# Attention outputs written by feature and not normalised, divided later in the dense stages; 4+3 PSUM banks for maxima and scores

## The chip, the cores and the metric

The kernel runs on one core of a Trainium2 chip. The metric is the device time of one execution in microseconds; the profiled execution is one such execution, and the trace quoted below is its trace. Engines: PE is TensorE, PEld its weight loads, DVE is VectorE, ACT is ScalarE, POOL is GpSimd, SP is SyncE, which issues every DMA of this kernel.

## The reference

The input x is (2, 2048, 256) in float32. There are 16 heads of 16 features.

```python
x = x + attn_a(layernorm(x))   # qkv = x @ W_attn; causal softmax; att * decay; y @ W_proj
x = x + ffn(layernorm(x))      # weights replaced by mean|w| * sign(w), exact gelu, 256 -> 1024 -> 256
x = x + attn_b(layernorm(x))   # biased q, k, v; causal softmax; o @ Wo + bo; layernorm * gamma + beta
x = x + ffn(layernorm(x))
```

In both attentions a query's output is a sum over keys of weight times value, divided by the sum of the weights. In the first the numerator's weights are multiplied by a table that falls with the distance and is 0 from 512 on, while the denominator sums all keys.

## The kernel before, in words

Six stages run one after the other, with a barrier between them: `setup` (signs of the FFN weights), `projections` (q, k, v of attention A), `attention` "att_a" (decayed), `dense` "mid" (A's output projection, FFN, q, k, v of attention B), `attention` "att_b", and `dense` "end" (B's output projection, its layernorm, FFN). They pass data through DRAM.

**attention** (L544 to L923) works on 8 groups (2 sequences by 4 groups of 4 heads), on 4 chunks of 512 queries each. Two passes are interleaved by a written-out order, `attention_plan` (L456): for group g it runs scores and outputs, and beside them the maxima of the rest of g and of the first part of g+1. All engines walk the same list of items, each taking what is its own:
- "M": scores of 128 queries by up to 512 keys (PE, L860) into one of `MBANKS` banks of PSUM, and their row maximum (DVE, L782, L786). In att_a the keys that the decay leaves out also get "FX" (ACT, L749): exponentials summed into `fsum`, later corrected and added up into `ftotal` (L806, L809).
- "MC": the maxima are turned by DVE (L815) and written into the operand `qop` by DMA (L672), so that the scores come out shifted.
- "S": scores by key block (PE, L882) into one of `EBANKS` banks, exponentials (ACT, L742), in att_a the decay (POOL, L704).
- "PO" and "PV": sums of weights and weighted values, four heads in four strips of 32 partitions of the one bank `po` (L900, L907, L917). A strip holds 16 features and then rows with the sum of weights.
- "O": ACT copies `po` to `y` (L762). "YT": PE turns `y` by four transposes into the bank `px` (L869). "YN": DVE adds `ftotal` where there are far keys (L823), takes the reciprocal of a 128x16 tile (L825, L827), scales 128x256 values (L831), and SP stores them (L677), one DMA a chunk.

PSUM has 8 banks: 4+2 for maxima and scores in att_a, 3+3 in att_b, and one each for `po` and `px`.

**dense** (L1005 to L1434) works on 8 chunks of 512 rows, in the order of `dense_plan` (L934), which all engines walk. Its items: "Y" loads y (L1074), turns it by 8 transposes (PE, L1214) and copies it to `yt` (ACT, L1304); "P" projects (PE, L1232; DVE adds the residual, L1386, or the bias, L1380); "S", "N" and "T" are moments on DVE (L1348 on) with the normalising on POOL (L1143, L1151); "A" is a residual sum (DVE, L1395); "X" and "Z" are transposes; "H" is one of 8 blocks of the FFN's first matrix (PE, L1250; ACT's gelu, L1316; DVE splits it in two, L1409, L1411); "O" is its part of the second matrix (PE, L1261), which needs DVE's L1411; "B" and "R" turn back and add (L1269, L1419); "Q" and "V" are the next q, k, v. In mid, Y of chunk G+2 stands in the list after the third O of chunk G; in end, Y of chunk G+3 stands after the last O of chunk G and after "N". The list of either opens with a prologue:

```python
    plan = [("Y", 0), ("P", 0), ("S", 0), ("Y", 1)]
    if not qkv:
        plan += [("A", 0), ("N", 0)]
    plan += [("P", 1), ("S", 1), ("X", 0)]
    if not qkv:
        plan += [("A", 1), ("N", 1), ("Y", 2)]
    plan += [("H", 0, h) for h in range(EARLY)]
```

SP loads the first two chunks of y and x, the weights, and in mid last `wqkv`, `bqk` and `bv` (L1093 to L1097). In mid, DVE waits for these (`qkv_in`, L1366) before its first item.

## Time and profile before

| | us |
|---|---|
| median of 3 runs | 2737.45 (2736.65 to 2740.8) |
| profiled execution, its own time | 2736.11 |
| its span, first to last instruction | 2734.4 |
| PE busy | 2454.8 (90%) |
| DVE busy | 1958.3 (72%) |
| ACT busy | 1515.6 (55%) |
| POOL busy | 1052.5 (38%) |
| mean granted TensorE clock | 0.959 of full |

A busy time is the time in which an instruction of the engine is under way; PE's counts pipelined matmuls with modelled ends, so it is not work at its peak. A wait names the instruction that released it. Between two stages all engines stop.

### The profile page before, as it was taken

To read this page: it belongs to the slowest core of one execution; us is meant where nothing else is said; L and a number is where in the kernel's file an instruction comes from. 1 tells how busy PE (TensorE), PEld (TensorE's weight loads), DVE (VectorE), ACT (ScalarE), POOL (GpSimd) and SP (SyncE) were. 2 spreads that over 40 slices of the span, in tenths; PEclk is the share of its full clock that TensorE was granted. 3 is DMA by queue.
4 is the path that set the end of the run, shared out by engine and by line. 5 is a ranking of instruction groups with operands and counts; after the bars stand their busy time and mean duration, and the time that the engine had idled before them with its cause. 6 is when DMAs were issued, how large, how long until landed. Compare 5 with 4: busy or idle time off the path is not lost. (4 is left out here: it accounts for less than half of the span.)

```text
span 2734.4 us, 44488 instructions
## 1 busy us (share of the span) xinstructions
PE 2454.8 (90%) x13984; PEld 1404.0 (51%) x13984; DVE 1958.3 (72%) x4863; ACT 1515.6 (55%) x3309; POOL 1052.5 (38%) x1274
## 2 busy tenths in 40 slices
PE   4959999999999999969997599999999999997788
PEld 2535545454544545437774355555555555553676
DVE  5667787777787777716663588888888888870786
ACT  1218576776767685734332056666666666664333
POOL 0037777777777777751221301000101001011653
PEclk8969999999999999989998589999999999998999
DMA  4994142332505050033544751423505234102110
GB/s 134 252 144 63 24 56 36 44 51 32 70 11 75 13 69 6 5 114 77 125 96 98 111 75 16 64 38 44 70 15 72 32 51 62 18 7 99 47 54 31
DMA packets 181847, 171.03 MB, mean 63 GB/s; under 512 B 90352, under 2 KB 131056, under 8 KB 180848
## 3 DMA queue, kind: packets, MB, share of 16 engines
q1 hardware_dynamic: 181616, 168.18, 35.0%
q8 instruction: 116, 1.90, 0.3%
q14 instruction: 115, 0.94, 0.2%
HBM read 105.98 MB, written 61.08 MB: 61 GB/s over the span
## 5 line engine op out<-in xcount | busy, mean ns | idle before, releaser
L704 POOL TENSOR_TENSOR att_a_wd<-att_a_wt,decay 128x256 f32<-128x256 f32 (+3 forms) x896 | 754.6, 873 | 259.8 <-PE att_a_po L907 122.7
L742 ACT ACTIVATE att_b_wt<-att_b_ps 128x512 f32<-128x512 f32 (+3 forms) x1280 | 589.4, 539 | 354.6 <-PE att_b_ps L882 352.6
L782 DVE TENSOR_REDUCE att_a_mpart<-att_a_pm 128x1 f32<-128x512 f32 x768 | 513.5, 687 | 132.2 <-PE att_a_pm L860 129.0
L782 DVE TENSOR_REDUCE att_b_mpart<-att_b_pm 128x1 f32<-128x512 f32 x768 | 503.7, 686 | 109.7 <-PE att_b_pm L860 107.7
L860 PE MATMUL att_a_pm<-att_a_kop,att_a_qop 128*128 128x512 f32 (+3 forms) x1280 | 522.6, 426 | 55.6 <-DMA att_a_qop<-att_a_qop 28.2
L742 ACT ACTIVATE att_a_wt<-att_a_ps 128x512 f32<-128x512 f32 (+3 forms) x896 | 430.8, 506 | 218.1 <-PE att_a_ps L885 131.6
L860 PE MATMUL att_b_pm<-att_b_kop,att_b_qop 128*128 128x512 f32 (+3 forms) x1280 | 503.0, 408 | 36.6 <-DMA att_b_qop<-att_b_qop 29.9
L882 PE MATMUL att_b_ps<-att_b_qop,att_b_kop 128*128 128x512 f32 (+3 forms) x1280 | 453.2, 383 | 6.6 <-ACT att_b_wt L742 3.4
L722 POOL TENSOR_SCALAR_AFFINE_SELECT att_b_wt<-att_b_wt 128x512 f32<-128x512 f32 x128 | 81.6, 637 | 867.1 <-ACT att_b_wt L742 867.1
L860 PEld LDWEIGHTS att_a_pm<-att_a_kop,att_a_qop 128*128 128x128 f32 x1280 | 240.6, 193 | 324.6 <-DVE att_a_mpart L782 130.2
L860 PEld LDWEIGHTS att_b_pm<-att_b_kop,att_b_qop 128*128 128x128 f32 x1280 | 246.3, 194 | 277.1 <-DVE att_b_mpart L782 112.0
L882 PE MATMUL att_a_ps<-att_a_qop,att_a_kop 128*128 128x512 f32 (+3 forms) x896 | 324.2, 370 | 6.2 <-ACT att_a_wt L742 6.1
L749 ACT ACTIVATE att_a_pm<-att_a_pm,att_a_mpart 128x512 f32<-128x512 f32 x384 | 255.2, 665 | 95.5 <-DVE att_a_mpart L782 92.7
L917 PE MATMUL att_b_po<-att_b_wt,att_b_va 128*17 128x512 f32 (+3 forms) x2560 | 296.6, 535 | 11.0 <-ACT att_b_y L762 7.8
L786 DVE CUSTOM_DVE_ANT_0 att_a_pm<-att_a_pm,late 128x384 f32<-128x384 f32 (+3 forms) x512 | 248.3, 498 | 69.2 <-PE att_a_pm L860 69.1
L882 PEld LDWEIGHTS att_b_ps<-att_b_qop,att_b_kop 128*128 128x128 f32 x1280 | 234.2, 189 | 118.8 <-ACT att_b_wt L742 84.2
L786 DVE CUSTOM_DVE_ANT_0 att_b_pm<-att_b_pm,late 128x384 f32<-128x384 f32 (+3 forms) x512 | 248.5, 498 | 50.4 <-PE att_b_pm L860 49.2
L900 PE MATMUL att_a_po<-att_a_wt,ones_strip 128*32 128x512 f32 (+3 forms) x1792 | 198.6, 515 | 18.9 <-ACT att_a_y L762 18.9
L882 PEld LDWEIGHTS att_a_ps<-att_a_qop,att_a_kop 128*128 128x128 f32 x896 | 169.9, 190 | 75.3 <-ACT att_a_wt L742 63.4
L907 PE MATMUL att_a_po<-att_a_wd,att_a_va 128*16 128x256 f32 (+3 forms) x1792 | 164.1, 438 | 3.3 <-POOL att_a_wd L704 3.3
L885 PE MATMUL att_a_ps<-mask_k,identr 128*128 128x128 f32 x512 | 118.7, 236 | 0.0
L1143 POOL TENSOR_TENSOR mid_rs<-mid_var,mid_power 128x4 f32<-128x4 f32 x16 | 17.6, 1098 | 234.5 <-DVE mid_var L209 234.5
(174 smaller groups left out, 2622.6 us busy)
## 6 DMA issues: line engine op xcount, KB each, us to landing
att_a_kop<-qk SPq DMA_DIRECT2D x128, 128.0 KB, 7.7
att_a_qop<-qk SPq DMA_DIRECT2D x128, 128.0 KB, 8.0
att_b_kop<-qk SPq DMA_DIRECT2D x128, 128.0 KB, 6.2
att_b_qop<-qk SPq DMA_DIRECT2D x128, 128.0 KB, 6.8
qk<-qkv_a_qk_hi SPq DMA_DIRECT2D x32, 256.0 KB, 4.7
qk<-qkv_a_qk_lo SPq DMA_DIRECT2D x32, 256.0 KB, 4.5
qk<-mid_qk_hi SPq DMA_DIRECT2D x32, 256.0 KB, 4.0
qk<-mid_qk_lo SPq DMA_DIRECT2D x32, 256.0 KB, 4.5
```

Of the source, the lines that this page charges most:

```text
L704: pool.tensor_tensor(wd[:, kq % 2, j, a:z], wt[:, kq % buffers, j, a:z], keep["decay"][:, u:u + z - a], ALU.mult).then_inc(w_decayed, 1)
L722: pool.affine_select(out=block, in_=block, compare_op=ALU.is_ge, fill=0.0, base=0, pattern=[[0, GH], [1, P]], channel_multiplier=-1).then_ ...
L742: act.activation(wt[:, kq % buffers, j, a:CH], pe_[:, seen % EBANKS, 0:CH - a], ACT.Exp)\
L749: act.activation(pm[:, n % MBANKS, :], pm[:, n % MBANKS, :], ACT.Exp, bias=mpart[:, c, piece, u:u + 1], accum_out=fsum[:, c, piece, u:u + ...
L782: dve.tensor_reduce(mpart[:, c, piece, u:u + 1], pm[:, n % MBANKS, 0:w], AX.X, ALU.max, negate=True).then_inc(m_reduced, 1)
L786: dve.tensor_tensor_reduce(out=pm[:, n % MBANKS, 0:w], in0=pm[:, n % MBANKS, 0:w], in1=keep["late"][:, CH - w:CH], scale=-1.0, scalar=-2 * ...
L860: mm = pe.matmul(pm[:, bank, 0:w], qop[:, mpar, c, j, qb * P:(qb + 1) * P], kop[:, mpar, j, piece * CH:piece * CH + w], start=True, stop=True)
L882: mm = pe.matmul(pe_[:, bank, 0:CH - a], kop[:, par, j, kb * P:(kb + 1) * P], qop[:, par, c, j, a:CH], start=True, stop=not diagonal)
L885: mm = pe.matmul(pe_[:, bank, 0:P], keep["identr"][:, :], keep["mask_k"][:, :], start=False, stop=True)
L900: mm = pe.matmul(po[STRIP * j:STRIP * (j + 1), a:CH], keep["ones_strip"][:, :], wt[:, ones % buffers, j, a:CH], start=first, stop=False)
L907: mm = pe.matmul(po[STRIP * j:STRIP * j + VW, a:z], va[:, par, kb, j, :], wd[:, kq % 2, j, a:z], start=False, stop=last)
L917: mm = pe.matmul(po[STRIP * j:STRIP * j + VW, a:CH], va[:, par, kb, j, :], wt[:, kq % buffers, j, a:CH], start=first, stop=last)
```

## The change

Both attentions no longer transpose or divide their output. "YT" and "YN" are gone from the plan. At "O" ACT copies `po` into one of two buffers `y`, and SP stores it as it lies, 8 DMAs a chunk (for each head 16 feature rows, and one row of sums). In att_a the far sums are turned by DVE, 16 at a time ("FT"), and stored by 4 DMAs to a tensor of their own. The bank `px` goes to the others: 4+3 in both attentions. In the dense stages y comes by feature, so PE's transposes and ACT's copy of "Y" are gone. Instead SP loads each head's sums spread over 16 partitions (16 DMAs a chunk, 16 more where there are far sums, that is in mid for chunks 2, 3, 6 and 7, which POOL adds), and DVE takes the reciprocal of 128x1024 values and multiplies.

```diff
 def attention_plan(...):
-            follow(number + 3, GH - 1, ("YT", c))
...
-    return [x for item in plan for x in ((item, ("YN", *item[1:])) if item[0] == "YT" else (item,))]
+    return [item for _, _, _, item in sorted(timed)]
 def spaced(m, decayed):
-                follow((8, 0.0, ("FE", c)), (11, 0.0, ("FM", c)))
+                follow((8, 0.0, ("FE", c)), (11, 0.0, ("FM", c)), (14, 0.0, ("FT", c)))
 def attention(...):
-        MBANKS, EBANKS = (4, 2) if decayed else (3, 3)
+        MBANKS, EBANKS = 4, 3
...
+        y = sb("y", [P, 2, CH], F32)
+        pm, pe_, po = ps("pm", [P, MBANKS, CH]), ps("ps", [P, EBANKS, CH]), ps("po", [P, CH])
...
         SP:
+                    if item[0] == "FT":
+                        sp.wait_ge(f_turned, len(FARS) * (g + d) + n + 1)
+                        for k in range(P // SQUARE):
+                            sp.dma_start(to[:, k, :], frow[SQUARE * k:SQUARE * k + UNITS, n, :]).then_inc(f_out[n], 16)
-                    if item[0] == "YN":
+                    if item[0] == "O":
+                        sp.wait_ge(o_kept, done(g, c) + 1)
+                        for j in range(GH):
+                            sp.dma_start(dram["y"][g // NG, h, :, cols], y[STRIP * j:STRIP * j + HD, c % 2, :])\
+                              .then_inc(y_out[c % 2], 16)
+                            sp.dma_start(dram["sums"][g // NG, h:h + 1, cols],
+                                         y[STRIP * j + HD:STRIP * j + HD + 1, c % 2, :]).then_inc(y_out[c % 2], 16)
...
         ACT, item "O":
+                        act.wait_ge(y_out[c % 2], Y_DMAS * (2 * g + c // 2 + 1))
+                        act.activation(y[:, c % 2, :], po[:, :], ACT.Copy).then_inc(o_kept, 1)
...
         DVE:
+                    if item[0] == "FT":
+                        dve.transpose(frow[:, n, :], ftotal[:, n, :]).then_inc(f_turned, 1)
-                    if item[0] == "YN":  (L816 to L832)
         PE:
-                    if item[0] == "YT":  (L863 to L870)
 def dense(...):
             def load_y(G):
                 if G >= 2:
-                    sp.wait_ge(y_turned, G - 1)
+                    sp.wait_ge(yt_ready, G - 1)
+                sp.dma_start(y[:, G % 2, :, :], dram["y"][b].rearrange("(k h) d t -> (h d) k t", k=KT)[:, :, cols])\
+                  .then_inc(y_in[G % 2], 16)
+                for h in range(H):
+                    sp.dma_start(sums[part, G % 2, h // (H // KT), :],
+                                 dram["sums"][b, h:h + 1, cols].to_broadcast([HD, CH])).then_inc(y_in[G % 2], 16)
+                if G in FAR_CHUNKS:
+                    if n:
+                        sp.wait_ge(sums_ready, n)
+                    for h in range(H):
+                        sp.dma_start(far_sums[part, h // (H // KT), :], row_of(row).to_broadcast([HD, CH]))\
+                          .then_inc(far_in, 16)
...
         POOL:
+                if item[0] == "Y" and G in FAR_CHUNKS:
+                    pool.tensor_tensor(sums[:, G % 2, :, :], sums[:, G % 2, :, :], far_sums[:, :, :], ALU.add)\
+                        .then_inc(sums_ready, 1)
         PE:
-                if item[0] == "Y":  (transposes, L1221 to L1224)
         ACT:
-                if item[0] == "Y":  (copy, L1300 to L1304)
         DVE:
+                if item[0] == "Y":
+                    dve.wait_ge(y_in[par], Y_LOADS * (G // 2 + 1))
+                    if G in FAR_CHUNKS:
+                        dve.wait_ge(sums_ready, FAR_CHUNKS.index(G) + 1)
+                    if G:
+                        dve.wait_ge(projected, G)
+                    dve.reciprocal(sums[:, par, :, :], sums[:, par, :, :]).then_inc(inverted, 1)
+                    dve.wait_ge(inverted, G + 1)
+                    dve.tensor_tensor(yt[:, :, :], y[:, par, :, :], sums[:, par, :, :], ALU.mult).then_inc(yt_ready, 1)
```

## Rows read from the trace of the kernel before

**Rows 1.** Windows by stage: us, busy time and instructions of PE, PEld, DVE, ACT, POOL, clock, DMA

```profile
168.00:1188.00 1020.00, 961.19 (x6360) 505.64 (x6360) 780.20 (x1989) 696.61 (x1709) 760.19 (x896) 0.98 0.31 41
1520.00:2498.00 978.00, 928.08 (x5224) 487.66 (x5224) 758.24 (x1924) 602.71 (x1308) 101.31 (x138) 0.96 0.33 46
```

**Rows 2.** Windows of one steady chunk of mid and one of end, columns as in Rows 1

```profile
1269.70:1303.60 33.90, 32.73 (x146) 24.03 (x145) 21.33 (x49) 13.22 (x17) 8.17 (x13) 1.00 0.58 121
2603.30:2627.50 24.20, 21.77 (x106) 17.15 (x104) 19.87 (x43) 9.42 (x12) 13.76 (x15) 1.00 0.20 66
```

**Rows 3.** Timeline, end, a steady chunk: start us, us, engine, line, instruction, [idle before <-releaser]

```profile
2625.43 0.42 DVE L1409 CAST end_g_hi<-end_g 128x512 fp32r<-128x512 f32 x1
2626.64 0.73 PE L1261 MATMUL end_po<-end_g_hi,end_w_signs 128*128 128x512 f32 x2 [0.28 <-DVE end_g_lo L1411]
```

**Rows 4.** Groups by line: the output transposes of the attentions, busy, mean ns, idle before

```profile
L869 PE MATMUL att_b_px<-ident,att_b_y 128*128 128x128 f32 x128 | 20.0, 279 | 3.1 <-ACT att_b_y L762 3.1
L869 PE MATMUL att_a_px<-ident,att_a_y 128*128 128x128 f32 x128 | 19.6, 275 | 2.7 <-ACT att_a_y L762 2.7
```

**Rows 5.** Timeline of PE in a steady stretch of att_b

```profile
2005.60 0.62 PE L869 MATMUL att_b_px<-ident,att_b_y 128*128 128x128 f32 x4
2005.97 0.47 PE L860 MATMUL att_b_pm<-att_b_kop,att_b_qop 128*128 128x512 f32 x1
```

**Rows 6.** Waits: who waited for whom, total us, times, longest us

```profile
PEld att_b_pm L860 <- DVE att_b_mpart L782: 112.0, 241, 0.9
PEld att_a_ps L882 <- ACT att_a_wt L742: 63.4, 121, 2.4
```

**Rows 7.** Timeline, issues of SP: a load of 16 partitions, the spread load of bv

```profile
158.39 0.43 SPq L646 DMA_DIRECT2D att_a_kop<-qk  x1
1209.09 0.71 SPq L1097 DMA_DIRECT2D mid_bv<-in_L_attn_b_bv  x1
```

**Rows 8.** Groups by line: reciprocals and whole-chunk elementwise work on VectorE

```profile
L323 DVE RECIPROCAL qkv_a_rs<-qkv_a_sd 128x4 f32<-128x4 f32 x8 | 1.4, 178 | 2.3 <-ACT qkv_a_sd L377 2.3
L825 DVE RECIPROCAL att_a_inverse<-att_a_sums 128x16 f32<-128x16 f32 x16 | 4.0, 253 | 0.6
L1395 DVE TENSOR_TENSOR end_x<-end_zg,end_xb 128x1024 f32<-128x1024 f32 x8 | 9.7, 1215 | 10.6 <-POOL end_zg L1171 10.6
L771 DVE MEMSET att_a_mneg<- 128x64 f32 x1 | 0.1, 112 | 0.1
L1163 POOL TENSOR_TENSOR end_xb<-end_x,end_beta 128x1024 f32<-128x1024 f32 x8 | 19.3, 2409 | 9.5 <-DMA end_beta<-in_L_attn_b_beta 9.5
```

**Rows 9.** Timeline, opening of mid

```profile
1197.57 0.36 SPq L1074 DMA_DIRECT2D mid_y<-y  x1
1204.72 5.53 PE L1232 MATMUL mid_pp<-mid_wp,mid_yt 128*128 128x256 f32 x16 [1.21 <-ACT mid_yt L1304]
1214.88 0.17 DVE L1367 TENSOR_SCALAR mid_bqk<-mid_bqk 128x2 f32<-128x2 f32 x1 [20.36 <-DMA mid_bv<-in_L_attn_b_bv]
1227.98 0.47 PE L1250 MATMUL mid_ph<-mid_xt_hi,mid_w_signs 128*128 128x512 f32 x1 [4.00 <-DVE mid_xt_lo L1401]
```

**Rows 10.** Timeline, a steady chunk of mid

```profile
1294.78 0.69 DVE L1411 TENSOR_TENSOR mid_g_lo<-mid_g,mid_g_hi 128x512 fp32r<-128x512 f32 x1
1300.02 3.62 PE L1232 MATMUL mid_pp<-mid_wp,mid_yt 128*128 128x256 f32 x16
1301.19 1.40 DVE L1348 BATCH_NORM_STATS2 mid_stats<-mid_x 128x6 f32<-128x256 f32 x4
1303.32 0.16 DVE L209 SCALAR_TENSOR_TENSOR mid_var<-mid_half 128x4 f32<-128x4 f32 x1
1307.84 1.09 PE L1214 MATMUL mid_pt<-ident,mid_xn 128*128 128x128 f32 x8 [0.53 <-POOL mid_xn L1151]
```

**Rows 11.** Timeline, opening of end: the first load, and the first product with W2

```profile
2506.47 0.36 SPq L1074 DMA_DIRECT2D end_y<-y  x1
2551.68 0.74 PE L1261 MATMUL end_po<-end_g_hi,end_w_signs 128*128 128x512 f32 x2 [2.62 <-DVE end_g_lo L1411]
```

More of the change, by code:

```diff
@@ L862, in step @@
                         mm.then_inc(m_scores, 1)
-                    if item[0] == "YT":
-                        c = item[1]
-                        pe.wait_ge(o_kept, done(g, c) + 1)
-                        if done(g, c) > 1:
-                            pe.wait_ge(y_ready, done(g, c) - 1)
-                        for t in range(TB):
-                            mm = pe.transpose(px[:, t * P:(t + 1) * P], y[:, t * P:(t + 1) * P], keep["ident"][:, :])
-                        mm.then_inc(y_turned, 1)
                     if item[0] == "S":
@@ L1066, in dense @@
         N_W = 16 * (1 + 3 * bool(norm))
+        Y_LOADS, F_LOADS = 16 * (1 + H), 16 * H
+        FAR_CHUNKS = [G for G in range(CHUNKS) if decayed and far(G % NC, decayed)]
         N_QKV = 16 * (len(weights) + 3) if qkv else 0
@@ L1197, in wait_turned @@
                     what, G = BEFORE[item]
-                    if what == "Y":
-                        pe.wait_ge(yt_ready, G + 1)
-                    elif what == "X":
+                    if what == "X":
                         pe.wait_ge(hi_ready, G + 1)
@@ L1459, in build @@
             "v": dram("v", (B, NG, NC, P, TB * GH * (HD + 1)), F32),
-            "y": chunks(dram("y", (B, T, D), F32)),
+            "y": dram("y", (B, H, HD, T), F32),
+            "sums": dram("sums", (B, H, T), F32),
+            "far": dram("far", (B, NG, NC, UNITS, P), F32),
             "w1s": dram("w1s", (P, KT, FF), F32), "w2s": dram("w2s", (P, HT, D), F32),
@@ L1480, in build @@
         attention(nc, "att_b", False, keep, scratch)
-        dense(nc, "end", x[1], x[2], t["L0_attn_b_Wo"], [t[f"L0_attn_b_{n}"] for n in ("bo", "gamma", "beta")],
+        dense(nc, "end", x[1], x[2], t["L0_attn_b_Wo"], False, [t[f"L0_attn_b_{n}"] for n in ("bo", "gamma", "beta")],
               None, None, keep, scratch)
```

88 lines of the change are left out of this document (39 added, 49 removed).

## The prediction

> **What bounds the kernel now.** I read the windows by stage first, since an average over stages hides what each part of the change meets. The two attentions hold 1998 of 2734 us. In both PE has something under way for 94% and 95% of the time, DVE for 76% and 78% [rows 1]: PE sets the pace, so work taken off PE counts, and work taken off DVE counts only through what PE waits for. Next came the windows of one chunk of each dense stage. In mid PE is busy 32.7 of 33.9 us, DVE 21.3. In end PE is busy 21.8 and DVE 19.9 of 24.2 us [rows 2], and the timeline says that DVE is the one behind: PE stands waiting for L1411, the split of a gelu block, right after DVE has come out of its moments [rows 3]. So end is paced by DVE and PE in turns, and anything that holds DVE at that place holds PE.
>
> The change thus takes work from PE in the stages that PE bounds, and puts work on DVE in the stages where DVE is near the bound or in the way. Sums are made against the profiled execution, 2736.1 us; the median of the runs is 1.3 us above it. About 0.2% (5.5 us) is what a measurement of this kernel can tell from no change.
>
> **Attentions: transposes and division.** There are 64 chunks (8 groups by 4 chunks, twice), each with 4 transposes. From the first of them to the next instruction of PE is 0.37 us [rows 5], so 64 x 0.37 = 24 us, plus PE's idle time before them, 3.1 + 2.7 us [rows 4]: **-30**. Their busy time, 20.0 and 19.6 us, overlaps the neighbours and would be the upper price (-45). DVE's adds, reciprocals and scalings go too, some 0.8 us a chunk; PE is the bound, so they are costed at nothing beyond the waits of the next part. DVE's 16 transposes of the far sums come in their place, about 0.2 us each by the transpose of the maxima, hidden in the same way.
>
> **Attentions: banks.** att_a gets a third scores bank, att_b a fourth maxima bank. The waits that they bear on are PE's weight loads for ACT's exponentials (63.4 us in att_a) and for DVE's maxima (112.0 us in att_b) [rows 6]. A weight load may be early, so most of such a wait lies beside the matmul before it. Bounds: 0 (PE had other work), and all the time in which PE has nothing under way, 59 + 50 us [rows 1], less the 6 already counted, so -103. I take a third: **-36**, nearer the lower end, as the waits are 0.5 us on average and PE is over 94% busy.
>
> **Attentions: stores.** SP issues 8 DMAs a chunk for one, 0.43 us each by the nearest row, a DMA of 16 partitions [rows 7]. That is 3.4 us of SP in some 30 us, plus 4 small ones for each of the 16 far chunks. Behind them on SP stand the writes of the maxima into qop (L672) and the next group's loads; SP is mostly waiting there, so they cost nothing, and if that cover is gone PE's first score of a chunk waits for L672. At the end of a stage there is no cover: 7 more issues are 3.0 us, less about 1.5 for the transposes and division that stood there. Twice: **+3**.
>
> **What Y costs on DVE.** This decides the case. Reciprocals of 4 elements a partition take 178 ns and of 16 take 253 [rows 8]: 75 ns for 12 elements, 6.25 ns each, over a fixed 153. For 1024 elements that is 153 + 1024 x 6.25 = 6550 ns. An addition of the same size takes 1.22 us for all of it [rows 8], so a reciprocal pays about five times as much per element. With the multiplication, 1.22, and a gap, Y is **7.85 us** of DVE, 16 times. Bounds: 2.5 us, if a long reciprocal ran as an addition; and 10.3, if the fixed part were only the 112 ns of the shortest memset [rows 8], since (253 - 112) / 16 = 8.8 ns, 9.1 us for 1024. I take 7.85, because it alone fits both sizes of this very operation.
>
> The Trainium skill's page "VectorE: DVE Perf Modes" (First, the fixed hardware budget) says that the reciprocal is an iterated division with a repeat count of 8. Eight cycles at the 0.96 GHz of that page would be an estimate of 8.3 ns an element, where the rows give 6.25; what that would make of the time is a rival below.
>
> **Opening of mid.** SP issues everything in order. Y of chunks 0 and 1 becomes 17 DMAs each, so 32 more stand ahead of `bv`, the last thing that DVE waits for. Before, the first load went out at 1197.6, `bv` at 1209.1, and DVE started at 1214.9 [rows 7, 9]. Now there are about 45 issues, at 0.43 to 0.46 us some 21 us and 1 us for the slower ones, so `bv` goes out near 1220 and DVE starts near 1225: +10 (bounds +3, if the issues before were waiting for data, as 8.7 us for the last seven suggest, to +20 at the 0.71 of `bv` [rows 7]). Then DVE's Y stands in line. Before, the projection of chunk 0 was long done when DVE began, and the first FFN block ran 13.1 us later [rows 9]. Now Y(0) comes first, then the projection, 5.53 us [rows 9], then Y(1): 7.85 + 5.53 + 7.85 = 21. Together **+31**.
>
> **Steady mid.** Y(G+2) follows a split that ended at 1295.5 [rows 10], so it ends at 1303.3. PE goes on meanwhile with blocks whose splits are done, and loses its own Y transposes; then it stands before P(G+2), which began at 1300.0. That is 3.3 late. DVE then has two splits, R and the moments T to do; T ran from 1301.2 to 1303.5 [rows 10] and would now end near 1309.0 (1303.3 + 1.1 + 1.2 + 1.1 + 2.3). POOL normalises from T, and PE's Z, at 1307.84, waited for it already by 0.5 us [rows 10]. So Z and all after it slip by **5.5** a chunk, six times (chunks 2 to 7): **+33**. What is late next is POOL's chain from T to Z. DVE had 12.6 us of slack a chunk [rows 2], which is why not all 7.85 shows. POOL's addition of the far sums, 2.4 us [rows 8], four times, lies where POOL waits anyway; if DVE's two-input work collides with it, it costs up to 2 us each.
>
> **Opening of end.** The first load goes out at 2506.5 [rows 11]; 17 issues (7.5) and a landing (2 to 3) bring the data by 2516.5. I replay the list with 5.5 for a projection, 3.6 for an addition and its moments (1.2 + 2.3), and about 6 for POOL's chain (1.0 + 0.2 + 2.2 for normalising, 2.4 for gamma). Y(0) to 2524, P(0) to 2530, S(0) to 2533, Y(1) to 2541 with POOL's chain beside it, A(0) and N(0) to 2545 with P(1) beside, S(1) to 2550, X(0) to 2553, A(1) and N(1) to 2560 after POOL's second chain, Y(2) to 2567.5, the split to 2568.6. Then PE's first product with W2 starts; before it was at 2551.7 [rows 11]: **+17** (10 to 22).
>
> **Steady end.** Y(G+3) stands between the moments N and the split that PE is waiting for [rows 3]. Nothing of it is hidden: PE's next product waits all of it, then R, then P, which needs R's banks. The chain after it is the same as before, shifted. The floor is DVE's own work, 19.9 + 7.85 against 24.2, so +3.5; the ceiling is 7.85. I take 7.7, five times (chunks 3 to 7): **+38**. After such a wait PE's clock is low: the projection took 5.53 us after a wait and 3.62 in full swing [rows 9, 10]. It follows close on the stall and lies on the path: 1.5 us five times, **+8** (0 to 10).
>
> **Sum.** -30 - 36 + 3 = -63 for the attentions; 31 + 33 = +64 for mid, 17 + 38 + 8 = +63 for end. Together +64: 2736.1 + 64 = 2800.
>
> **Rivals.**
> (a) *The long reciprocal is cheap* (Y is 2.5 us). Then mid's opening costs 10 + 2.5 + 5.5 + 2.5 = 20.5, its six chunks gain 1.4 each (the transposes and the wait before them), end pays 3 + 5 x 2.5 = 15.5: +27 in all, against -63: 2700. For it: every other DVE operation here pays about 1.2 ns an element. Against: two sizes of the same operation [rows 8]. Between 2700 and 2800 the sum crosses zero where Y is about 4.4 us. Chance 0.08.
> (b) *The banks free PE fully*: -103 instead of -36 gives 2733, just faster or the same. For it: DVE and ACT have 20% and more to spare in both attentions. Against: every step there goes in fixed order, and no wait of PE is long. Chance 0.08, half of it faster.
> (c) *A long reciprocal costs more an element than the short ones*: Y at the upper bound's 8.8 ns is 10.3 us, 2.4 more, and all 16 lie on the path: 2800 + 39 = 2839. Against: the slope of 6.25 between two sizes [rows 8]. Chance 0.12. (By the page's eight cycles, in the Trainium skill's "VectorE: DVE Perf Modes", the estimate would be 2.1 more for each, 2834.)
> (d) *SP becomes the bound in mid*. A far chunk has 33 loads, 12 stores and 2 more; at 0.43 this is 20 us of 39, at 0.71 33 us, and the loads wait in order behind `yt_ready`. If spread loads issue slower still, DVE waits for y: another 20 to 35 us, 2825. Against: SP's unhindered issues are all near 0.43. Chance 0.12.
> (e) *The banks bring nothing*: 2836. Chance 0.06.
>
> **How the numbers follow.** The forecast has 0.54; the rivals 0.08, 0.08, 0.12, 0.12, 0.06. Its own range, from the bounds of the two openings, of the banks and of the end chunks, is 2765 to 2830. The range 2744 to 2845 leaves out (a), (b) and the top of the slower cases. Faster: (a) and half of (b), 0.12 less what is left of them within 0.2%: 0.11. Same: 0.03. Slower: 0.86.
>
> **What would show it.** Right: a reciprocal of 128x1024 near 6.5 us, 16 of them; PE waiting in end for L1411 by 7 us right after; mid's DVE starting near 1225 less what att_a gained; mid some 64 us longer, end some 63; each attention some 30 shorter, with no L869, and PE's waits for L782 and for L742 smaller. Wrong: a reciprocal near 1.2 us (a); attentions shorter by over 50 each (b); SP issuing without a pause through mid while DVE waits for a DMA of sums (d).

## The result, and the profile after

The changed kernel takes **2834.7 us** (median of 4 runs, 2831.0 to 2837.7) where the kernel before takes 2738.0 (2736.7 to 2740.8): a ratio of 1.0351, with a 95% interval of 1.0333 to 1.0369. That is 97 us slower. The forecast was 64 us slower, 2800 us, and its range of 2744 to 2845 holds the result. The profiled execution took 2837.7 us, with a span of 2836.0 and a mean granted clock of 0.929.

I cut the span into stages at the first load that each stage issues. The stage starts of the changed kernel, from SP's queue in the timeline (start us, us, engine, line, instruction):

```profile
155.83 0.33 SPq L648 DMA_DIRECT2D att_a_kop<-qk  x1
1174.19 0.38 SPq L1077 DMA_DIRECT2D mid_y<-y  x1
1584.10 0.34 SPq L648 DMA_DIRECT2D att_b_kop<-qk  x1
2536.56 0.38 SPq L1077 DMA_DIRECT2D end_y<-y  x1
```

The same cuts in the kernel before lie at 156.6, 1197.6, 1531.2 and 2506.5. So each stage took, in us:

| stage | before | after | difference | forecast |
|---|---|---|---|---|
| first attention | 1041.0 | 1018.4 | -22.6 | -31 |
| mid | 333.7 | 409.9 | +76.3 | +64 |
| second attention | 975.3 | 952.5 | -22.8 | -31 |
| end | 227.9 | 299.4 | +71.5 | +63 |

A stage that an edit doesn't touch varies between executions by about 1 to 3 us (the second attention by 7), so differences of a few us in one stage say little.

Windows of the changed kernel, columns as in [rows 1]: the attentions, then one steady chunk of mid and one of end, which answer to [rows 2].

```profile
168.00:1165.00 997.00, 947.75 (x6238) 492.64 (x6239) 763.65 (x1928) 691.85 (x1709) 758.71 (x895) 0.98 0.33 43
1596.00:2529.00 933.00, 906.28 (x5103) 482.70 (x5103) 730.58 (x1856) 600.99 (x1308) 89.31 (x132) 0.97 0.34 46
1319.90:1360.60 40.70, 33.63 (x138) 24.72 (x137) 28.54 (x53) 12.33 (x17) 7.46 (x12) 0.92 0.56 129
2663.20:2697.20 34.00, 23.97 (x97) 18.24 (x96) 27.21 (x45) 8.49 (x11) 12.32 (x14) 0.85 0.22 62
```

PE is busy for 95.1% of the first attention's window, where it was 94.2%. The second attention needs care: its window before, in [rows 1], opens at 1520, while the stage's first load goes out at 1531.2 and its first matmul starts at 1543.05:

```profile
1543.05 7.20 PE L860 MATMUL att_b_pm<-att_b_kop,att_b_qop 128*128 128x128 f32 x16 [28.52 <-DMA att_b_qop<-att_b_qop]
```

So 23 of the 50 us without PE work that [rows 1] shows there are the stage's opening. From 1543.2 to 2498 PE was busy for 97.2%, and it is 97.1% now: that attention is shorter because PE has less under way, not because it idles less. In the dense stages PE waits more than before. A chunk of mid went from 33.9 to 40.7 us with PE busy for 33.6 us where it was 32.7, and DVE is busy for 28.5 us of it, 7.2 more than before. A chunk of end went from 24.2 to 34.0, with 7.3 us more of DVE and a granted clock of 0.85 where it was 1.00.

**What Y costs.** The groups by line (busy us, mean ns of one | idle before), which answer to the estimate from [rows 8]:

```profile
L1393 DVE RECIPROCAL mid_sums<-mid_sums 128x1024 f32<-128x1024 f32 x8 | 52.4, 6547 | 0.0
L1393 DVE RECIPROCAL end_sums<-end_sums 128x1024 f32<-128x1024 f32 x8 | 52.4, 6551 | 61.4 <-DMA end_sums<-sums 61.4
L1395 DVE TENSOR_TENSOR mid_yt<-mid_y,mid_sums 128x1024 f32<-128x1024 f32 x8 | 9.8, 1225 | 0.3
L1180 POOL TENSOR_TENSOR mid_sums<-mid_sums,mid_far_sums 128x1024 f32<-128x1024 f32 x4 | 9.6, 2402 | 0.0
```

The reciprocal is 6.55 us, as forecast, and the multiplication 1.22.

**Opening of mid**, timeline, to be held against [rows 9]:

```profile
1202.15 6.55 DVE L1393 RECIPROCAL mid_sums<-mid_sums 128x1024 f32<-128x1024 f32 x1
1210.11 5.80 PE L1249 MATMUL mid_pp<-mid_wp,mid_yt 128*128 128x256 f32 x16 [41.31 <-DVE mid_yt L1395]
1227.29 5.76 PE L1249 MATMUL mid_pp<-mid_wp,mid_yt 128*128 128x256 f32 x16 [11.38 <-DVE mid_yt L1395]
1237.92 0.47 PE L1267 MATMUL mid_ph<-mid_xt_hi,mid_w_signs 128*128 128x512 f32 x1 [4.00 <-DVE mid_xt_lo L1422]
```

DVE's first Y, Y(0), starts 28 us after the stage's first load, P(0) comes after it, then Y(1), then P(1). The first FFN block comes 63.7 us after the first load; before it came after 30.4.

**A steady chunk of mid**, to be held against [rows 10]:

```profile
1319.88 6.55 DVE L1393 RECIPROCAL mid_sums<-mid_sums 128x1024 f32<-128x1024 f32 x1
1322.35 0.61 PE L1278 MATMUL mid_po<-mid_g_lo,mid_w_signs 128*128 128x512 f32 x2
1326.46 1.23 DVE L1395 TENSOR_TENSOR mid_yt<-mid_y,mid_sums 128x1024 f32<-128x1024 f32 x1
1328.66 1.22 DVE L1440 TENSOR_TENSOR mid_x<-mid_pp,mid_x 128x1024 f32<-128x1024 f32 x1
1330.03 5.58 PE L1249 MATMUL mid_pp<-mid_wp,mid_yt 128*128 128x256 f32 x16 [7.07 <-DVE mid_x L1440]
```

PE ends its last product with W2 at 1322.96 and then stands for 7.07 us. What it needs is R (L1440), which empties the banks of `pp` and stands behind Y and one split on DVE. Then the projection P takes 5.58 us, at a granted clock of 0.66 in the window 1330.0 to 1335.6; before it took 3.62, at 1.00 [rows 10]. PE's waits of 0.5 us before, for POOL's normalised x at Z, and of 0.6 us for DVE are gone.

**A steady chunk of end**, to be held against [rows 3]:

```profile
2663.16 6.55 DVE L1393 RECIPROCAL end_sums<-end_sums 128x1024 f32<-128x1024 f32 x1
2672.09 1.22 PE L1278 MATMUL end_po<-end_g_hi,end_w_signs 128*128 128x512 f32 x2 [8.00 <-DVE end_g_lo L1432]
2673.11 1.05 PE L1278 MATMUL end_po<-end_g_lo,end_w_signs 128*128 128x512 f32 x2
2674.38 5.83 PE L1249 MATMUL end_pp<-end_wp,end_yt 128*128 128x256 f32 x16 [0.22 <-DVE end_x L1440]
```

Here PE's product with W2 waits 8.00 us for the split behind Y. The products after the stall take 1.22 and 1.05 us where such a pair of matmuls takes 0.62 to 0.73 in the steady chunks before the change, and the projection 5.83 where those chunks had 3.69. The granted clock is 0.50 from 2672.0 to 2674.4, 0.62 from 2674.4 to 2680.0 and 1.00 in the 4 us behind; "the low clock" below means the level of 0.50, for the whole of a stretch or for a part of it. The slow products cost nothing here: from the start of the first to the start of the projection it is 2.29 us now and was 2.29 us before (2626.64 to 2628.93), as the projection waits for R on DVE in both. So a chunk's 9.85 us more are 7.7 of stall (8.00 for 0.28 us) and 2.1 of the projection.

### The profile page after: what moved, and what is told of

The parts are those of the page before. It is cut to its first block and busy times, and to the rows that moved or that the text cites. A ratio compares the mean times of both kernels' runs of the same rounds, so it can differ in the third digit from the quotient of the medians.

```text
span 2836.0 us, 44312 instructions
## 1 busy us (share of the span) xinstructions
PE 2430.7 (86%) x13600; PEld 1390.1 (49%) x13600; DVE 2038.0 (72%) x4768; ACT 1495.0 (53%) x3293; POOL 1047.8 (37%) x1278
## 5 line engine op out<-in xcount | busy, mean ns | idle before, releaser
L866 PE MATMUL att_a_pm<-att_a_kop,att_a_qop 128*128 128x512 f32 (+3 forms) x1280 | 511.2, 425 | 59.9 <-DMA att_a_qop<-att_a_qop 28.6
L866 PE MATMUL att_b_pm<-att_b_kop,att_b_qop 128*128 128x512 f32 (+3 forms) x1280 | 486.6, 401 | 36.8 <-DMA att_b_qop<-att_b_qop 30.8
L880 PE MATMUL att_b_ps<-att_b_qop,att_b_kop 128*128 128x512 f32 (+3 forms) x1280 | 460.7, 386 | 12.2 <-DMA att_b_qop<-att_b_mrow 7.1
L866 PEld LDWEIGHTS att_a_pm<-att_a_kop,att_a_qop 128*128 128x128 f32 x1280 | 239.1, 194 | 309.3 <-DVE att_a_mpart L799 131.7
L866 PEld LDWEIGHTS att_b_pm<-att_b_kop,att_b_qop 128*128 128x128 f32 x1280 | 246.2, 195 | 252.5 <-DVE att_b_mpart L799 108.6
L880 PEld LDWEIGHTS att_b_ps<-att_b_qop,att_b_kop 128*128 128x128 f32 x1280 | 238.4, 189 | 129.5 <-ACT att_b_wt L757 77.8
L880 PEld LDWEIGHTS att_a_ps<-att_a_qop,att_a_kop 128*128 128x128 f32 x896 | 170.5, 191 | 84.5 <-ACT att_a_wt L757 71.1
L1328 ACT ACTIVATE end_g<-end_ph,b,alpha 128x512 f32<-128x512 f32 x64 | 49.9, 779 | 168.8 <-PE end_ph L1267 164.1
L1328 ACT ACTIVATE mid_g<-mid_ph,b,alpha 128x512 f32<-128x512 f32 x64 | 49.9, 779 | 155.2 <-PE mid_ph L1267 155.2
```

Of the source, the lines that this page charges most:

```text
L866: mm = pe.matmul(pm[:, bank, 0:w], qop[:, mpar, c, j, qb * P:(qb + 1) * P], kop[:, mpar, j, piece * CH:piece * CH + w], start=True, stop=True)
L880: mm = pe.matmul(pe_[:, bank, 0:CH - a], kop[:, par, j, kb * P:(kb + 1) * P], qop[:, par, c, j, a:CH], start=True, stop=not diagonal)
L1328: act.activation(g[:, h % GB, :], ph[:, BANK[item], :], ACT.Gelu, bias=keep["b1"][:, h:h + 1], scale=keep["alpha1"][:, h:h + 1]).then_inc( ...
```

## The experiments

All are edits of the changed kernel, but for the control. The table gives the median of all runs, the ratio to the kernel before (to runs of it made beside each kernel, with medians of 2738.0 to 2738.9) with its interval, and the stages of the profiled execution, cut as above (us).

| kernel | median | ratio | att_a | mid | att_b | end |
|---|---|---|---|---|---|---|
| before | 2738.0 | 1 | 1041.0 | 333.7 | 975.3 | 227.9 |
| changed | 2834.7 | 1.0351 [1.0333, 1.0369] | 1018.4 | 409.9 | 952.5 | 299.4 |
| no reciprocal | 2725.9 | 0.9954 [0.9935, 0.9974] | 1018.5 | 349.1 | 946.6 | 254.5 |
| banks of before | 2856.7 | 1.0424 [1.0407, 1.0441] | 1026.8 | 410.8 | 963.7 | 298.4 |
| other banks | 3012.9 | 1.0991 [1.0973, 1.1010] | 1090.9 | 411.5 | 1052.5 | 299.0 |
| four pieces | 2811.5 | 1.0277 [1.0246, 1.0308] | 1018.5 | 397.2 | 952.2 | 285.8 |
| scaling later | 2816.8 | 1.0276 [1.0259, 1.0293] | 1018.2 | 392.5 | 953.4 | 298.4 |
| Y of end after S | 2822.6 | 1.0304 [1.0286, 1.0323] | 1018.1 | 408.6 | 946.6 | 286.1 |
| Y of mid after block 6 | 2846.3 | 1.0395 [1.0380, 1.0410] | 1016.8 | 420.8 | 952.5 | 298.5 |
| compact inverse | 2734.8 | 0.9984 [0.9970, 0.9997] | 1026.2 | 343.6 | 951.8 | 252.7 |
| compact, two orders | 2716.4 | 0.9912 [0.9895, 0.9928] | 1026.3 | 332.8 | 955.1 | 244.4 |
| and two spread loads | 2707.1 | 0.9886 [0.9871, 0.9900] | 1026.7 | 327.8 | 952.2 | 240.9 |
| control: before, scaling later | 2734.2 | 0.9983 [0.9975, 0.9992] | 1042.8 | 327.1 | 974.4 | 231.2 |

### No reciprocal

```
-                    dve.reciprocal(sums[:, par, :, :], sums[:, par, :, :]).then_inc(inverted, 1)
-                    dve.wait_ge(inverted, G + 1)
```

> The changed kernel without its 16 long reciprocals: Y multiplies by the sums, so the division is left out. Theory (a reciprocal lies on the path with its whole 6.55 us, and PE's low clock behind the stall with 1.5 to 2 us): both openings shorter by 13 and 14 us, mid's steady chunk 33.5 instead of 40.7 us (six times, -43), end's steady chunk 26 instead of 34.0 us (five times, -40): about -110, 2725 us. Rival 1 (the 17 to 33 loads of a chunk through SP, or the place of Y in the order, cost by themselves): at most half of it comes back, 2780 us or more. Rival 2 (the reciprocal costs its duration and nothing more, 16 times): -95 to -105 with the projection still at 5.4 us after a wait, 2735 us.

Measured: 2725.9 us, 109 less than the changed kernel, where the 16 reciprocals last 104.8 together. The theory's 2725 holds in the sum, and rival 1 (at most half comes back) falls. The theory's parts fit less well: mid gave 60.8 us where 56 were expected and end 45.0 where 54 were, and 5.9 us come from the second attention, which the edit leaves alone. So the sum alone does not tell the theory from rival 2, by which a reciprocal costs its duration and nothing more; the stages and the projections do. The projections, on PE in the timeline, a chunk of mid and one of end:

```profile
1294.81 3.69 PE L1249 MATMUL mid_pp<-mid_wp,mid_yt 128*128 128x256 f32 x16 [0.49 <-DVE mid_x L1438]
2611.22 5.33 PE L1249 MATMUL end_pp<-end_wp,end_yt 128*128 128x256 f32 x16 [1.35 <-DVE end_x L1438]
```

In mid the stall is down from 7.07 to 0.49 us, the projection is back at 3.69 (granted clock 1.00), and a chunk takes 32.4 us (from the starts of R), 1.5 less than before the change. In end a chunk takes 27.2 us, 3.0 more than before, and the projection stays at 5.33, at a granted clock of 0.68, as rival 2 had it. Two short stalls stand ahead of it, 1.43 for a split and 1.35 for R, where the kernel before had 0.28 and 1.10 and a projection of 3.69. So one multiplication of 1.22 us at that place goes with 3.0 us more a chunk, of which 1.6 are the slow projection.

### The banks

```
-        MBANKS, EBANKS = 4, 3
+        MBANKS, EBANKS = (4, 2) if decayed else (3, 3)
```

> The changed kernel with the banks of before: 4 for maxima and 2 for scores in the first attention, 3 and 3 in the second. The rest of the change stays. The attentions got 45 us shorter together where 63 was forecast. Theory (the banks are worth only what is left after 30 for the transposes): +15 to +18, 8 in each attention, 2852 us, with PE's waits for the exponentials and the maxima nearly unchanged in number. Rival 1 (the banks are worth the 36 of the forecast, and the stores cost some 20): +36, 2871 us. Rival 2 (the banks are worth nothing, and the transposes cost 45 with their busy time): 2835 us, no change.

Measured: 2856.7, 22 us more than the changed kernel, from 8.4 in the first attention and 11.2 in the second. This is nearer the theory (2852) than either rival (2871 and 2835). What is left between this kernel and the kernel before is the removal of the transposes and of the division, with the new stores: -14.2 and -11.6, together -26, where the forecast had -30 + 3. So these two terms were right in their sum (no run takes them apart), and the banks' was not. The second attention varies by up to 7 us between kernels that are the same there, so its 11.2 and 11.6 are rough; the two medians, 2856.7 and 2834.7, confirm some 20 us for both banks. The waits of this kernel (us in total, times, longest):

```profile
PEld att_b_pm L866 <- DVE att_b_mpart L799: 130.4, 252, 0.9
PEld att_a_ps L880 <- ACT att_a_wt L757: 98.9, 193, 1.4
```

and of the changed kernel:

```profile
PEld att_b_pm L866 <- DVE att_b_mpart L799: 108.6, 161, 0.9
PEld att_a_ps L880 <- ACT att_a_wt L757: 71.1, 104, 1.2
```

The extra bank takes 21.8 us off the first wait and 27.8 off the second, and the stages got 11.2 and 8.4 shorter, a half and a third of that. Against the kernel before [rows 6], 112.0 and 63.4, the waits of the changed kernel hardly fall or even rise: without its transposes PE comes earlier to the same waits. Only these two kernels, which differ in the banks alone, show what a bank is worth. PE's time from a stage's first matmul to the stage's end, by windows of the three traces (us with an instruction under way, us without):

| kernel | first attention | second attention |
|---|---|---|
| before | 964.5, 64.8 | 930.9, 32.5 |
| banks of before | 962.1, 52.8 | 922.4, 29.3 |
| changed | 950.1, 56.2 | 907.6, 32.9 |

With the extra bank the time without an instruction does not fall, it rises by 3.4 and 3.6 us; what falls is the time under way, by 12.0 and 14.8. The weight loads' waits for a bank, 130.4 us for the maxima of the second attention alone, are longer than the 29.3 us without an instruction there, so most of them lie beside matmuls that count as under way.

Then the splits on the other side:

```
-        MBANKS, EBANKS = 4, 3
+        MBANKS, EBANKS = (3, 4) if decayed else (5, 2)
```

> The changed kernel with other splits of the seven banks: 3 for maxima and 4 for scores in the first attention, 5 and 2 in the second. Read by stage. Theory (each attention is within a few per cent of PE's own work, and 4 and 3 is near the best): both attentions longer, the first by 5 to 15 us, the second by 3 to 15: 2850 us. Rival (the waits for the maxima, the larger ones in the second attention, show that banks for maxima are what it lacks): the second attention shorter by 5 or more.

Measured: +72.5 in the first attention and +100.0 in the second. The theory expected 5 to 15 and 3 to 15 us. The direction was right, but the sizes are some 5 and 7 times the tops of these ranges. The rival (the second attention shorter by 5 or more) falls. Waits:

```profile
PEld att_b_ps L880 <- ACT att_b_wt L757: 252.5, 658, 1.0
PEld att_a_pm L866 <- DVE att_a_mpart L799: 200.1, 315, 1.5
PE att_a_pm L866 <- ACT att_a_pm L764: 46.3, 113, 1.0
```

With two banks for scores in the second attention, PE's weight loads wait 658 times for an exponential, 252.5 us where it was 77.8 (157 times). The first attention, with two banks for scores, lost only 8.4; with three for maxima it loses 72. There PE waits 200.1 us for DVE's maxima (131.7 in the changed kernel) and 46.3 us for ACT's exponentials of the far scores, which also hold these banks (8.3). So of the splits tried 4 and 3 is the best for both attentions, but two banks can be nearly enough in one stage and far too few in the other.

### The reciprocal in four pieces

The items `("I", G, k)` take a piece of 256 elements each and stand between earlier splits; the multiplication stays where Y was.

```
+                if item[0] == "I":
+                    k = item[2]
...
+                    part = sums[:, par, k // 2, k % 2 * 256:k % 2 * 256 + 256]
+                    dve.reciprocal(part, part).then_inc(inverted, 1)
```

> The changed kernel with each reciprocal cut into four of 256 elements (1.75 us each by the fixed part and slope, 7.0 in all), which stand one by one at earlier places of the order, between the splits of the FFN blocks; the multiplication stays where Y was. VectorE has the same work and 0.5 us more a chunk. Theory (in mid it is the stall of PE behind one long instruction that costs, VectorE has 12 us of slack there; in end the sum of VectorE's work is nearly the bound): mid's chunk 35 to 36 instead of 40.7 us, end's chunk 29 to 30 instead of 34.0: -50, 2785 us. Rival (the amount of VectorE's work decides, not the length of one instruction): within 10 us of the changed kernel, 2835 to 2845 us.

Measured: 2811.5, 23 less than the changed kernel and not 50. Both stages gave about 13 us. Rows of two chunks of mid and one of end, from the timeline:

```profile
1369.38 1.75 DVE L1407 RECIPROCAL mid_sums<-mid_sums 128x256 f32<-128x256 f32 x1 [2.88 <-POOL mid_sums L1188]
1339.13 5.37 PE L1309 MATMUL mid_ph<-mid_xt,mid_wqkv 128*128 128x512 f32 x8 [3.31 <-DVE mid_qk_lo L1459]
2688.58 5.33 PE L1257 MATMUL end_pp<-end_wp,end_yt 128*128 128x256 f32 x16 [3.08 <-DVE end_x L1452]
```

A piece takes 1.75 us, so the slope from 256 to 1024 elements is (6.55 - 1.75) / 768 = 6.25 ns, and the fixed part 0.15: the same line as between 4 and 16 elements. In a near chunk of mid (1320.7 to 1358.2) PE waits only 0.7 us before the projection, which is back at 3.69. But the chunk takes 37.5 us where the kernel without a reciprocal has 32.4, because the stall has moved: PE's qkv products wait 3.31 us for DVE's split of them (L1459), which stands behind two pieces, and 8 of them then take 5.37 us at a granted clock of 0.68, where the 8 before took 3.60. A far chunk takes 41, since its first piece waits 2.88 us for GpSimd's addition. In end the projection is still slow after a stall of 3.08, and a chunk takes 31.3 to 33.3 where 29 to 30 were expected. So neither the theory nor the rival (within 10 us of the changed kernel) stands alone. Cutting the instruction gives back a fifth of what the reciprocal costs (23 of 109 us); the rest goes with the amount of work, since most of DVE's idle time in mid is time in which it owes something within a few us.

### Where Y stands

In end, after the moments S:

```
                 if h == 3 and ahead:
                     plan.append(("S", G + 2))
+                if h == 3 and G + 3 < CHUNKS:
+                    plan.append(("Y", G + 3))
...
                 if h == 7 and ahead:
                     plan.append(("N", G + 2))
-                if h == 7 and G + 3 < CHUNKS:
-                    plan.append(("Y", G + 3))
```

> The changed kernel with the full Y (reciprocal and multiplication) of end after the moments S instead of after the moments N; nothing else. Theory (6.55 us of VectorE in one instruction hold PE wherever they stand between two splits, since end has no long stretch of PE without a split): end's chunk 32.5 to 34 instead of 34.05 us: -8 to 0, 2830 us. Rival (it is the place ahead of R and P that costs): end's chunk below 31 us, -15 or more, 2820 us or less.

Measured: 2822.6, with end 13.3 us shorter; a chunk takes 31.1 to 32.6. It lies between the two. A projection in the steady stretch:

```profile
2661.94 3.61 PE L1249 MATMUL end_pp<-end_wp,end_yt 128*128 128x256 f32 x16
```

It takes 3.61, at a granted clock of 1.00, where the changed kernel has 5.83, and a chunk gained 2.3 us on average. But the low clock is not gone. The same 6.55 us of DVE still hold PE, which stands idle for 8.8 us ahead of 2649.16, and what follows the stall is now a block of the FFN and its product: these eight matmuls take 3.56 us at a granted clock of 0.50, and the next eight of the same kind take 1.87 at 0.98. So the same instructions on the same data show what the low clock costs, 2.2 us for a projection and 1.7 for a block; how the 2.3 us of a chunk divide among this and the waits is open.

In mid, Y after block 6 of the chunk, where DVE was idle:

```
-                if h == 2 and ahead:
-                    plan.append(("Y", G + 2))
+                if h == 2 and G == 0:
+                    plan.append(("Y", 2))
...
+                if h == 6 and G + 3 < CHUNKS:
+                    plan.append(("Y", G + 3))
```

> The changed kernel with Y of mid moved: Y of chunk G+3 stands after block 6 of chunk G, ahead of the transposes and the qkv products, where VectorE was idle in the changed kernel, and not before R and P, behind which PE stood 7.07 us. Same work. Theory (PE's stall and the low clock behind it are the cost, the amount of VectorE's work is not, with 12 us of slack a chunk): mid's chunk 36 to 38 instead of 40.7 us, the projection at 3.7 instead of 5.6 to 5.9: -20, 2815 us. Rival (PE's qkv products wait for VectorE's splits, so the stall moves there with all its length): mid's chunk within 1.5 us of 40.7, 2830 us or more.

Measured: 2846.3, 12 us slower than the changed kernel. My theory fell, and the rival's mechanism holds. Near chunks take 40.3 and 40.6 us, as the rival has it; the two far chunks behind them take 45.1 and 44.7, more than it allowed. Rows of a far chunk:

```profile
1373.70 3.62 PE L1251 MATMUL mid_pp<-mid_wp,mid_yt 128*128 128x256 f32 x16
1388.86 6.55 DVE L1395 RECIPROCAL mid_sums<-mid_sums 128x1024 f32<-128x1024 f32 x1 [5.09 <-POOL mid_sums L1182]
1398.54 6.01 PE L1303 MATMUL mid_ph<-mid_xt,mid_wqkv 128*128 128x512 f32 x8 [10.65 <-DVE mid_qk_lo L1449]
```

The projection is at 3.62 again and no longer waits. But DVE waits 5.09 us for GpSimd's addition of the far sums before it can take the reciprocal, and PE's qkv products then stand 10.65 us for DVE's split of them (L1449) and run at a granted clock of 0.60, 6.01 us for 8 matmuls where 8 took 3.60 at 1.00 just before. In a near chunk, without the addition, they stand 5.47 us and 8 of them take 6.35 or 6.71. DVE's idle time at this place was not free: the first of those splits was due at 1386.9, when ACT had written `qk_hi`, before the reciprocal had begun.

### The opening of mid

```
-            if qkv:
-                dve.wait_ge(qkv_in, N_QKV)
...
                 if item[0] == "S":
                     dve.wait_ge(p_read, G + 1)
                     moments(z if norm else x1[:, G % 3, :, :])
+                    if qkv and G == 1:
+                        dve.wait_ge(qkv_in, N_QKV)
...
```

> The changed kernel with one wait moved: in mid VectorE waits for the qkv weights and biases and scales them after the moments of chunk 1, no longer ahead of all its work, so Y of chunk 0 can start when its 17 loads have landed. Theory (mid's opening is late by the queue of 33 loads ahead of these weights and by two serial Y): the first FFN block 46 us after mid's first load instead of 64, the rest of mid the same: -17, 2818 us. Rival (the 16 loads of the second chunk's sums are then the next wait, and Y of chunk 1 starts no earlier): -10 or less, 2825 us or more.

Measured: 2816.8 and mid 17.4 us shorter, with the first FFN block 46.4 us after the first load. So the theory holds, and the wait for these weights, behind the queue of loads, was worth 17 us to the changed kernel. The control, the same edit in the kernel before:

> A control: the kernel before, with only the scaling of mid's qkv weights moved after the moments of chunk 1. There the projection of chunk 0 ended at 1210.2 and VectorE began its addition at 1215.4, so theory: at most 5 us, with the second projection earlier by as much: -3 to -5, 2734 us. Rival (the edit is worth as much here as the 18 us in the changed kernel): -15, 2723 us, and then most of what the fastest version gains over the kernel before is not due to the change.

Measured: 2734.2, 4 us less, as the theory has it. In the profiled executions mid is 6.6 us shorter, a little more than the theory's 5, and end, which the edit leaves alone, 3.3 longer. The wait cost little there, since P(0) did not stand behind it.

### Dividing in compact form

The sums of a group's chunk are 4 x 512 numbers, which is 16 a partition. The kernel loads them back one chunk later, adds the far sums, inverts them there, and the dense stages spread the inverses.

```
+                if q >= 4:
+                    dve.wait_ge(ci_out[q % 4], 16 * (q // 4))
+                dve.reciprocal(ci[:, q % 4, :], cs[:, q % 4, :]).then_inc(c_inverted, 1)
...
-                    dve.reciprocal(sums[:, par, :, :], sums[:, par, :, :]).then_inc(inverted, 1)
-                    dve.wait_ge(inverted, G + 1)
                     dve.tensor_tensor(yt[:, :, :], y[:, par, :, :], sums[:, par, :, :], ALU.mult).then_inc(yt_ready, 1)
```

> Another way to divide: the attentions keep the stores by feature, 4+3 banks, and no transposes of the output; one chunk later the 4x512 sums of a group are loaded back as 128x16, the far sums are added to them there, VectorE takes a reciprocal of 128x16 (0.25 us), and the inverses are stored; the dense stages spread the inverses over partitions instead of the sums and only multiply (1.22 us). No far loads or additions on GpSimd in mid. Theory: the dense stages run as without the reciprocal, and the attentions keep their gain less 5 us at the end of each for the last round trip: about 2730 us. Rival (SP's three more transfers a chunk and VectorE's waits for them hold PE in the attentions): 2760 us or more.

Measured: 2734.8 against a theory of 2730; the rival (2760 or more) falls. The end of the first attention:

```profile
1174.76 0.34 SPq L661 DMA_DIRECT2D inverse<-att_a_ci  x1
1177.04 2.15 SPq L661 DMA_DIRECT2D inverse<-att_a_ci  x3
1177.72 0.25 DVE L884 RECIPROCAL att_a_ci<-att_a_cs 128x16 f32<-128x16 f32 x1
```

32 reciprocals of 0.25 us an attention take the place of 8 of 6.55. The last one has no cover: from the start of PE's last matmuls to the first load of mid it is 10.9 us, where the changed kernel has 5.8. That is 5.1 of the 7.8 us by which the first attention is longer than in the changed kernel. The second attention shows none of it beyond its variation.

Then the two orders of above in this kernel (scaling later in mid, and Y of end, now one multiplication, after S):

> The kernel with the inverses taken from 128x16 in the attentions, and two orders changed: VectorE scales the qkv weights in mid after the moments of chunk 1, and Y of end (now one multiplication) stands after the moments S instead of after the moments N, where PE waits for the split behind it. Theory: mid's opening shorter by 10 to 15; end's steady chunk back from 27.2 to 24.5 us, and the projection there at 3.7 instead of 5.3 us, since PE's stalls are short again (five times, -13): 2708 us, faster than before by 1.1%. Rival (end is held by VectorE's own work and its collisions with GpSimd, not by the place of Y): end's chunk stays at 26.5 or more, 2720 us.

Measured: 2716.4, where 2708 was expected. Mid gave 10.8 us. End gave 8.3 and not 13: a chunk takes 25.3 us, with the projection back at a granted clock of 1.00:

```profile
2581.66 3.69 PE L1298 MATMUL end_pp<-end_wp,end_yt 128*128 128x256 f32 x16
```

And the 16 spread loads of a chunk as two, with the inverses laid out by head:

```
-                for h in range(H):
...
+                for k in range(KT):
+                    rows = dram["inverse"][b, c, H // KT * k:H // KT * (k + 1), :]
+                    sp.dma_start(sums[:, G % 2, k, :],
+                                 rows.unsqueeze(1).to_broadcast([H // KT, HD, CH])).then_inc(y_in[G % 2], 16)
```

> The fastest version so far (inverses from 128x16, scaling later, Y of end after S) with one edit: the 16 spread loads of a chunk, one a head, become 2, each of 8 heads by 16 partitions by 512. Theory (SP's queue of 17 issues ahead of everything else sets both openings): first projection 5 to 6 us earlier in mid and in end, steady chunks unchanged: -11, 2705 us. Rival (a transfer of 128 rows of 2 KB from 8 rows of DRAM lands later than 8 small ones, by the bytes and not by the issues): no gain, 2716 us.

Measured: 2707.1, 9 us less. The opening of mid:

```profile
1182.53 1.37 SPq L1131 DMA_DIRECT2D mid_sums<-inverse  x2
1189.75 1.23 DVE L1436 TENSOR_TENSOR mid_yt<-mid_y,mid_sums 128x1024 f32<-128x1024 f32 x1 [10.72 <-DMA mid_sums<-inverse]
1191.12 5.99 PE L1299 MATMUL mid_pp<-mid_wp,mid_yt 128*128 128x256 f32 x16 [19.65 <-DVE mid_yt L1436]
```

Two issues take 1.37 us where 16 took 7.4, but the data are there only at 1189.75, 5.9 us after the second issue; the small ones of the kernel without this edit landed in 2.3 to 3.1 (medians of end and mid). So the first projection came 2 us earlier in mid and 4 in end, not 5 to 6, and the rival took a part of the gain there. That the total of 9 is still near the 11 of the theory has a part that it did not name: mid's second projection came 3.5 us earlier, and mid as a whole is 5.0 us shorter.

This version is 1.1% faster than the kernel before (0.9886, 0.9871 to 0.9900). Of its 31 us, 4 would come without the change, by the control. Whether the other order, Y of end after S, would gain anything in the kernel before was not tested.

## Why the prediction was right

The sign and the range held, and so did the mechanism in its main part: a reciprocal of 6.55 us on DVE holds PE, and costs the dense stages more than the attentions gain. The size was off by a third. All its misses go the same way, so that nothing cancelled. Step by step, in the stages of the two profiled executions (101.6 us between the spans, 64 forecast):

- **Transposes and division out of the attentions, stores in: -30 + 3.** Right as a sum: -26, by the kernel with the banks of before.
- **Banks: -36.** This term was mis-sized: -20. I took a third of PE's whole idle time, 59 + 50 us. That bound was read wrong: 23 of the 50 are the opening of the second attention, before its first matmul at 1543.05, and without them and the 6 already counted it is 80, a third of which is 27. (A third of the 103 that I had written is 34, not 36.) And the quantity was the wrong one: with the extra banks PE's time without an instruction rose by 3.4 and 3.6 us, and its time under way fell. What an extra bank takes off is 22 to 28 us of waits a stage, and a third to a half of it reaches the stage's end. The sign that I had named, smaller waits for L782 and L742, mostly failed: from 112.0 to 108.6 and from 63.4 to 71.1 against [rows 6], because these waits move when PE's other work goes.
- **Y: 7.85 us.** Right to 0.1. The line through two small sizes of the same operation [rows 8] held at 256 and at 1024 elements. Rivals (a) and (c) fall with it. The Trainium skill's page "VectorE: DVE Perf Modes" (First, the fixed hardware budget) speaks of a repeat count of 8, by which I had estimated 8.3 ns an element; the runs show 6.25, so the measurement decides over that estimate.
- **Opening of mid: +31.** Right: 63.7 less 30.4 is +33.3. Its parts are confirmed too: 13.2 of it are gone without the reciprocals, 17.4 with the scaling moved.
- **Steady mid: +5.5 a chunk, +33.** Mis-sized: 6.8 a chunk, +43 for all after the first FFN block. Here the path was wrong as well, and it is luck that 5.5 is near 6.8. I let PE be 3.3 late for P and followed Z through POOL's chain, 5.5 late. The trace shows PE standing 7.07 us, for R behind Y, and then a projection of 5.3 to 5.9 us at the low clock, 2.0 more in the chunk shown; at Z it no longer waits at all. Against these 9.0 stand PE's old waits of 0.5 and 0.6 and its transposes of y, about 1, which are gone. The clock I had put into end alone.
- **Opening of end: +17.** Right: 64.6 less 45.2 is +19.3.
- **Steady end: +7.7 and 1.5 of clock, five times, +46.** Nearly right: +52. A chunk is 34.05 against 24.2, so 9.85. The stall is as forecast, 7.7; the clock was mis-sized, 2.1 us in the projection and not 1.5. That makes 49 for the five chunks; the last 3 us lie outside them.
- **SP (rival d)** fell: DVE waited for sums only in the opening of end, where the wait ran into the stage start, and in steady chunks the loads took 7.4 to 9.1 us of SP, 15 to 16 in a far chunk of mid, out of some 34 to 41. **Banks free PE fully (b)** and **banks bring nothing (e)** fall with the bank runs. The time of (e), 2836, is what was measured, but by another way: the banks gave 20, and the dense stages cost 20 more than forecast.

So the miss of 38 us is 16 of banks, 10 in mid's chunks, 6 in end's, 5 in the two openings and 1 in the transposes.

What stays open: why the clock stays high after one short stall in end and not after another, and how much of the second attention's variation of 7 us is in the numbers of single stages.

## What to carry to other kernels

Price an elementwise operation by its own rows at two sizes and by the elements of a partition, and do a division where its data are smallest: the same inversions took 6.55 us a chunk spread over partitions and 4 x 0.25 = 1 us before spreading, and the round trip through memory was hidden one chunk behind, but for some 5 us at the end of the first attention. Before sharing out an engine's idle time, take the stage's opening out of the window. A long instruction on an engine that feeds another in small pieces costs its whole length and the slow stretch that follows the stall, and the feeder's idle time is room for it only if nothing that it owes comes due meanwhile. What a bank is worth shows only between kernels that differ in the banks alone, and one bank fewer can cost several times what one more brings.

## What the runs showed of the hardware

**TensorE's clock after a stall.** 16 matmuls of a projection (128x256 each) took 3.61 to 3.69 us at a granted clock of 1.00, and 5.1 to 6.7 us where it was lower for a part of them (0.66 for 5.58 us, 0.55 for 6.70), a ratio up to 1.86. The length of the stall ahead does not tell which: in end of the compact kernel each chunk has stalls of 1.4 us for a split and of 1.35 us for R, and the projections behind them took from 3.69 to 6.70 us. In the kernel before, 0.28 and 1.10 us went with 3.69 in every chunk.

**Reciprocal.** 0.15 us plus 6.25 ns an element of a partition, at 4, 16, 256 and 1024 elements alike; the multiplication has 1.2 ns.

**VectorE beside GpSimd.** The first far addition of mid in the changed kernel:

```profile
1240.25 2.37 POOL L1180 TENSOR_TENSOR mid_sums<-mid_sums,mid_far_sums 128x1024 f32<-128x1024 f32 x1
1240.51 2.40 DVE L1430 CAST mid_g_hi<-mid_g 128x512 fp32r<-128x512 f32 x1 [2.73 <-ACT mid_g L1328]
```

The cast takes 2.40 us, where it mostly takes 0.42, and ends 0.3 us after GpSimd's addition. It has a single operand; the prediction had counted only two-input work among that which collides. The second far addition, at 1274.32, meets the subtraction L1432, which takes 2.75 us for 0.69, and the two in steady chunks (1385.86 and 1426.75) meet splits of qkv that read one operand from PSUM and take their usual 0.75. The Trainium skill's page "Advanced Engine Details and Errata" (GPSIMD Details) names the shared interface and says that it conflicts with VectorE's instructions in a two-port mode or with two operands in SBUF; the trace agrees if the cast runs in such a mode, which no run here shows.

**Spread loads.** A transfer of 32 KB to 16 partitions landed 1.8 to 3.1 us after its issue (medians of the kernels). Of those of 256 KB to 128 partitions, each of which replaced eight, the data were there 5.9 us after the second issue in mid's opening, beside other loads.
